# Operand places, order of the first and last pairs, and 512-column products in two halves, in a graph network kernel

## What is computed

```python
h = jnp.maximum(_layernorm(x, axis=-1), 0.0)
x = x + L0(h, adj)       # attention-weighted diffusion, K = 3
h = jnp.maximum(_layernorm(x, axis=-1), 0.0)
x = x + L1(h, adj)       # three graph convolutions
# L0:
Xw = X @ Wv + bv
sj = Xw @ aw[:d, 0]; si = Xw @ aw[d:, 0]
e = leaky_relu(sj[:, None, :] + si[:, :, None] + ab[0], 0.2)
alpha = A * exp(e); transition = alpha / (alpha.sum(-1) + 1e-12)
for k in range(3):
    H = H + Xk @ Wk[k] + bk[k]
    Xk = transition @ Xk
return relu(H)
# L1, three times (relu but for the last):
out = adj @ (x @ W) + b
```

## Time and profile before

| | us |
|---|---|
| median of 3 runs | 844.22 (843.95 to 844.86) |
| profiled execution | 844.0 |
| its span, first to last instruction | 842.2 |
| TensorE busy | 825.1 |
| VectorE busy | 716.8 |
| ScalarE busy | 683.8 |
| GpSimd busy | 506.4 |

### The profile page before, as it was taken

The page is one execution under the profiler, slowest core; times in us unless marked ns, Lnnn a source line. Parts: engine busy times, 40 slices in busy tenths (PEclk is TensorE's granted clock), DMA queues, the critical chain, the costliest instruction groups (busy, mean ns, idle before and its releaser), DMA issues.

```text
span 842.2 us, 20991 instructions
## 1 busy us (share of the span) xinstructions
PE 825.1 (98%) x6214; PEld 777.6 (92%) x6214; DVE 716.8 (85%) x2001; ACT 683.8 (81%) x1675; POOL 506.4 (60%) x591
## 2 busy tenths in 40 slices
PE   8699999999999999999999999999999999999996
PEld 6599999999999999999999999999999999999996
DVE  5788888888888888888888888888889889888872
ACT  3788888888888888888888888888888888888773
POOL 3456655665665665665665665665665665665553
PEclk9999999999999999999999999999999999999999
DMA  6143343343343343343343344344344344334101
GB/s 169 29 114 81 95 114 78 93 114 82 97 106 86 99 101 87 99 99 88 99 97 89 101 96 95 93 97 101 88 97 103 86 96 112 81 92 101 45 26 38
DMA packets 244780, 77.15 MB, mean 92 GB/s; under 512 B 202294, under 2 KB 236859, under 8 KB 244668
## 3 DMA queue, kind: packets, MB, share of 16 engines
q1 hardware_dynamic: 243580, 74.77, 37.2%
q10 hardware_dynamic: 1088, 1.05, 0.4%
HBM read 43.00 MB, written 32.77 MB: 90 GB/s over the span
## 4 chain that ended last, share of the span: by engine, by line
PE 95%; POOL 1%; issue 1%; DVE 1%; ACT 1%; DMA 0%; SPq 0%; ACTq 0%; POOLq 0%; DVEq 0%
PE bank L968 43%; PE bank_p L968 37%; PE bank_turned L968 7%; PE bank_T L968 5%; PE bank_T L991 2%; PE bank_p L1149 1%; POOL w_gcn_lo L425 0%; POOL rstd L381 0%; DMA bv_row<-in_L_gnn_bv 0%; POOL y__lo L390 0%; ACT y_full L612 0%; ACT y_hi L567 0%; DVE y_full L782 0%; DVE stats L680 0%; PE bank_turned L979 0%
## 5 line engine op out<-in xcount | busy, mean ns | idle before, releaser
L390 POOL TENSOR_TENSOR y__lo<-y_full,y__hi 128x256 fp32r<-128x256 f32 x256 | 182.8, 734 | 132.4 <-ACT y_full L612 132.4
L381 POOL TENSOR_TENSOR rstd<-veps,minus_half 128x2 f32<-128x2 f32 x128 | 111.2, 869 | 190.4 <-DVE veps L697 190.4
L968 PE MATMUL bank_p<-w_p_hi,h0T_hi 128*128 128x258 f32 (+1 forms) x512 | 177.7, 363 | 2.5 <-ACT h0T_hi L510 2.5
L968 PE MATMUL bank_p<-w_p_lo,h0T_hi 128*128 128x258 f32 (+1 forms) x512 | 167.4, 342 | 0.0
L968 PE MATMUL bank_p<-w_p_hi,h0T_lo 128*128 128x258 f32 (+1 forms) x512 | 142.4, 339 | 0.6 <-DVE h0T_lo L674 0.6
L968 PE MATMUL bank<-w_gcn_hi,y__hi 128*128 128x256 f32 x512 | 130.8, 290 | 1.6 <-ACT y__hi L612 1.3
L968 PE MATMUL bank<-w_gcn_lo,y__hi 128*128 128x256 f32 x512 | 124.9, 279 | 0.0
L612 ACT ACTIVATE y__hi<-bank,bias_col 128x256 fp32r<-128x256 f32 x256 | 119.9, 468 | 3.1 <-PE bank L968 3.0
L612 ACT ACTIVATE y_full<-bank,bias_col 128x256 f32<-128x256 f32 x256 | 120.7, 472 | 0.0
L968 PEld LDWEIGHTS bank_p<-w_p_hi,h0T_hi 128*128 128x128 f32 x512 | 97.4, 190 | 9.4 <-ACT h0T_hi L510 2.9
L968 PEld LDWEIGHTS bank_p<-w_p_lo,h0T_hi 128*128 128x128 f32 x512 | 97.6, 191 | 5.4
(11 more groups left out here) (104 smaller groups left out, 2289.7 us busy)
## 6 DMA issues: line engine op xcount, KB each, us to landing
x_in<-in_x SPq DMA_DIRECT2D x64, 256.0 KB, 3.0
x_new<-x_out SPq DMA_DIRECT2D x64, 256.0 KB, 2.2
h_rows<-h SPq DMA_DIRECT2D x61, 256.0 KB, 2.1
h_blocks<-h_rows SPq DMA_DIRECT2D x244, 64.0 KB, 2.5
adj_blocks<-in_adj SPq DMA_DIRECT2D x256, 32.0 KB, 2.0
w_raw<-in_L_gnn_Wk ACTq DMA_DIRECT2D x3, 256.0 KB, 6.0
w_raw<-in_L_gnn_W SPq DMA_DIRECT2D x3, 256.0 KB, 3.5
wv_raw<-in_L_gnn_Wv ACTq DMA_DIRECT2D x1, 256.0 KB, 3.9
```

What stands on the lines that cost most here:

```text
L381: pool.tensor_tensor(rstd[n][k % 2][:], veps[n][k % 2][:], minus_half[:], ALU.pow)\
L390: pool.tensor_tensor(y[n][1][:, c], y_full[n][:, c], plain(y[n][0][:, c]), ALU.subtract)\
L968: return pe.matmul(dst, stationary, moving, start=start, stop=stop, skip_group_check=True)
```

## The change

It does four things.

1. Places: the operands of products are declared first, moving ones from a kilobyte boundary on (a filler tensor ahead of them), stationary ones behind a filler of 64 bytes. The rows of `w_p2` and `p2` become 288 floats wide, of which 258 are used. `scratch` goes; the dot products write their unused result into `x_out`.
2. The first rounds: `aw` and `bv` are spread by the DMA itself; row products and copies go. Pair 1 is normalized and turned in round 0, pair 2 in round 1; the bias rows are spread behind ap; weight cuts, adjacency cuts and statistics of the first pairs move between the first three rounds; counts of `keep_busy` change, and two more calls stand in round 0.
3. The last rounds: for the last pair y1's parts are made before s3's, ay stands before z3, and the identity turns before m and z1 are 8 and 8 for 16 and 8.
4. Each product of 512 columns for p0 and p1 becomes two of 256 with the same stationary block.

```diff
-BUSY_FIRST, BUSY_BEFORE, BUSY_BETWEEN, BUSY_TAIL = 11, 7, 8, 16
+BUSY_FIRST, BUSY_BEFORE, BUSY_BETWEEN, BUSY_SCORES, BUSY_SUMS, BUSY_TAIL = 11, 14, 6, 4, 8, 8
+WIDE = D + P // 4
...
+        sb("up_to_a_kilobyte", [P, 3 * P // 4])
+        w_gcn = [None] + [hilo(f"w_gcn{n}", [P, C, D]) for n in range(1, K)]
+        w_p01 = hilo("w_p01", [P, C, 2 * D])
+        y1 = slots_hilo(2, "y1_", [P, G, D])
+        m = hilo("m", [P, C, G, P])
+        s3 = hilo("s3", [P, G, D])
+        adjT_full = [sb(f"adjT_full{n}", [P, G, P]) for n in range(4)]
+        w_p2 = hilo("w_p2", [P, C, WIDE])
+        p2 = slots_hilo(2, "p2_", [P, G, WIDE])
+
+        sb("half_a_block", [P, P // 8])
+        w_gcn[0] = hilo("w_gcn0", [P, C, D])
+        h0T = slots_hilo(2, "h0T", [P, G, C, P])
+        s2 = sb("s2", [P, G, D])
+        y = [hilo(f"y{n}_", [P, C, G, P]) for n in range(2)]
+        h1 = [sb(f"h1_{n}", [P, G, D]) for n in range(2)]
+        aT = slots_hilo(2, "aT", [P, G, P])
+        adjT = slots_hilo(4, "adjT", [P, G, P])
...
-            sp.dma_start(aw_row[:], aw.rearrange("(o d) x -> o (d x)", o=1)).then_inc(score_rows_in, 16)
-            sp.dma_start(bv_row[:], row(bv)).then_inc(score_rows_in, 16)
+            sp.dma_start(aw_bc[:], aw.rearrange("(h d) o -> o h d", h=2).to_broadcast([P, 2, D]))\
+              .then_inc(score_weights_in, 16)
+            sp.dma_start(bv_bc[:], row(bv).to_broadcast([P, D])).then_inc(score_consts_in, 16)
...
 # SyncE, round 1
+                if second(i):
+                    load_adj_blocks(3, 3)
...
 # GpSimd, one(i, k)
+                if first(i):
+                    power(0, 1, 1)
+                    power(0, 2, 2)
                 if b is not None:
                     power(1, b, k - LAG_B)
-                if b is not None and not second(i):
+                if i == 2:
+                    gcn_weights_low((2,))
+                    adjT_low(0, 0)
+                if b is not None and after(i, 3):
                     adjT_low(b, (k - LAG_B) % ROUND)
...
 # ScalarE, one(i, k)
-                if a is not None and a < ON_TENSOR:
-                    hT_high(a, k)
-                if first(i):
+                if first(i):
+                    hT_high(0, 0)
                     p01_weights_high()
-                    biases_copied()
...
                     exponentials(a, k)
+                    if first(i):
+                        first_norm(1, 1)
+                    if second(i):
+                        hT_high(2, 2)
                     p1_copy(a, k, 0)
...
+                if first(i):
+                    hT_high(1, 1)
+                    gcn_weights_high((0,))
+                    biases_copied()
...
+                if second(i):
+                    first_norm(3, 3)
+                if i == N_PAIRS - 1:
+                    y1_high(a, k)
                 if c is not None and not tail(i):
                     s3_high(c)
+                if a is not None and i < N_PAIRS - 1:
+                    y1_high(a, k)
+                if first(i):
+                    first_norm(2, 2)
...
 # VectorE, round 0
                 x_statistics(1, 1)
+                moments(0, 1, 1, lambda: None)
+                guard_variance(0, 1, 1)
                 turn_adj(0, 0)
+                shift(0, 1, 1)
                 p2_low(0, 0)
-                moments(0, 1, 1, lambda: attention(0, 0))
-                guard_variance(0, 1, 1)
+                attention(0, 0)
                 aT_low(0, 0)
-                shift(0, 1, 1)
+                x_statistics(2, 2)
+                moments(0, 2, 2, lambda: None)
+                guard_variance(0, 2, 2)
+                hT_low(1, 1)
...
                 p0_bias(0, 0)
+                turn_adj(1, 1)
+                x_statistics(3, 3)
...
 # TensorE
-                        last = matmul(bank_p[:, g, :], h0T[k % 2][a][:, g, c, :], w_p01[b][:, c, :],
-                                      c == 0 and (a, b) == (HI, HI), c == C - 1 and a == LO)
+                        for n in range(2):
+                            cols = slice(n * D, (n + 1) * D)
+                            last = matmul(bank_p[:, g, cols], h0T[k % 2][a][:, g, c, :], w_p01[b][:, c, cols],
+                                          c == 0 and (a, b) == (HI, HI) and n == 0, c == C - 1 and a == LO)
...
+                if i == N_PAIRS:
+                    ay_product(b, kb)
                 if d is not None and not tail(i - 1):
                     z3_product(d, kd)
-                if b is not None:
+                if b is not None and i < N_PAIRS:
                     ay_product(b, kb)
...
                 if first(i):
-                    pe.wait_ge(bias_rows_in, 16 * 2)
-                    matmul(bank_3[:, 0:D], ones[:], bk_rows[:], True, True).then_inc(bias_rows_spread, 1)
-                    matmul(bank_3[:, D:2 * D], ones[0:1, :], b3_row[:], True, True).then_inc(bias_rows_spread, 1)
+                    keep_busy(BUSY_SCORES)
                 if a is not None:
                     spread_scores(a, k)
+                if second(i):
+                    turn_h(2, 2)
...
                 if c is not None:
                     z2_product(c, kc)
+                if first(i):
+                    turn_h(1, 1)
...
+                    keep_busy(BUSY_SUMS, bank_2[:, 0:P])
```

More of the change, by code:

```diff
@@ L95, in slots @@
             return [sb(f"{name}{s}", shape, dt) for s in range(n)]
-        def slots_hilo(n, name, shape):
-            return [hilo(f"{name}{s}", shape) for s in range(n)]
         x_in = slots(X_SLOTS, "x_in", [P, G, D])
         adj_blocks = slots(4, "adj_blocks", [P, G, P])
-        adjT_full = slots(4, "adjT_full", [P, G, P])
-        adjT = slots_hilo(4, "adjT", [P, G, P])
         x1b = slots(4, "x1b", [P, G, D])
@@ L348, in one @@
                 turned = here(i, -2) if i >= ON_TENSOR - 2 else None
+                if second(i):
+                    load_adj_blocks(3, 3)
                 if turned is not None:
                     write_rows(turned, turned % ROUND)
-                if (n := here(i, -2)) is not None:
+                if (n := here(i, -2)) is not None and not second(i):
                     load_adj_blocks(n, n % ROUND)
@@ L868, in _ @@
             shift(0, 0, 0)
[L869 to L870 removed]
+            dve.wait_ge(score_weights_in, 16 * 2)
             for c in range(C):
@@ L907, in one @@
                     s3_low(d)
-                if a is not None and a < ON_TENSOR:
-                    hT_low(a, k)
                 if (n := early_norm(i)) is not None:
@@ L920, in one @@
                 if second(i):
-                    turn_adj(a, k)
+                    shift(0, 3, 3)
                 if b is not None:
@@ L972, in turn_h @@
                 pe.wait_ge(norm_made[0], i + 1)
-                if after(i, 2):
-                    pe.wait_ge(m_lo, i - 1)
-                elif not first(i):
+                if not first(i):
                     pe.wait_ge(hT_first_lo, i)
@@ L1008, in h_low_ready, with times_weights @@
                     pe.wait_ge(hT_lo, i - ON_TENSOR + 1)
-            def times_weights(hT, rows, w, dst, starts, passes=(False, True)):
+            def times_weights(hT, rows, w, cols, dst, starts, passes=(False, True)):
                 steps = [(g, c, a, b) for low in passes for g in range(G) for c in range(C)
@@ L1015, in times_weights @@
                     start = c == 0 and a == HI and b == HI and g in starts
-                    last = matmul(dst[g], rows(hT[a], g, c), w[b][:, c, :], start, a == LO and c == C - 1)
+                    last = matmul(dst[g], rows(hT[a], g, c), w[b][:, c, 0:cols], start, a == LO and c == C - 1)
                 return last
@@ L1161, in one @@
                 kb, kc, kd = (k - LAG_B) % ROUND, (k - LAG_C) % ROUND, (k - LAG_D) % ROUND
-                if a is not None and a < ON_TENSOR:
-                    turn_h(a, k)
                 if first(i):
+                    turn_h(0, 0)
                     keep_busy(BUSY_BETWEEN)
@@ L1190, in one @@
                     ap_product(a, k)
+                if first(i):
+                    pe.wait_ge(bias_rows_in, 16 * 2)
+                    matmul(bank_3[:, 0:D], ones[:], bk_rows[:], True, True).then_inc(bias_rows_spread, 1)
+                    matmul(bank_3[:, D:2 * D], ones[0:1, :], b3_row[:], True, True).then_inc(bias_rows_spread, 1)
+                    keep_busy(BUSY_SUMS, bank_2[:, 0:P])
                 if b is not None and tail(i):
```

107 lines of the change are left out of this document (37 added, 70 removed).

## The result

| | before | changed |
|---|---|---|
| median of the runs, us | 844.54 (843.95 to 844.88, 4 runs) | 838.36 (836.86 to 838.93, 4 runs) |
| profiled execution, us | 844.0 | 836.86 |
| its span, us | 842.2 | 834.7 |
| its mean granted clock | 0.996 | 1.000 |

The ratio is 0.993, with a 95% interval of 0.9909 to 0.995: the change saves 6.2 us, where 12.7 were forecast. The first line of the profile page answers to the earlier trace rows. There are 773 more products, nearly all of them the halves, and TensorE is as full as before.

A forecast was written before the change was run, and what follows sets the result against it. TensorE, busy 98% of the span, was taken as the bound, with a second path over aT_hi as long. From 844.0 us, 6.7 (steady rounds), 4.8 (head) and 1.1 (tail) came off: 831.4, say 831.5 us; range 826 to 840.

The forecast's parts named there:

- part (a) of the steady rounds: Operand places in every steady round: all products get z1's places modulo 128, so slow 256-column products fall to about 0.113 us.
- Segment A: Steady round from ap to ay, where TensorE alone decides: better places save 0.11 us per round.
- the first rival: Steady rounds: places do nothing or the 0.118 pace stays, gain 0 to 3 us, 838 to 840 us; chance 0.22.
- the 6.7 us: Forecast gain of the 61 steady rounds, 0.11 us each; bounds 3.1 and 9.2, zero if places are nothing.
- If z3 and ay stay at 0.118, 0.05: Low case for the stretch from ap to ay: z3 and ay unimproved, 0.05 us saved per round.
- Segment B: Steady round from ay to ap (second p2 pass, s2, p0/p1): saves 0.15 us, all given back waiting for aT_hi at ap.
- The third rival: Path over aT_hi moves with TensorE and isn't the bound: ay-to-ap gain counts, 9 us more, 822 us; chance 0.05.
- The split: p0/p1 in steady rounds: 24 products of 256 columns for 12 of 512, weight loads hidden, worth nothing.
- The head: First rounds: spreads at about 13.5, 25.2 and 38 us; 5.4 us worked out, 4.8 taken, bounds 2.5 and 6.
- The second rival: First rounds: the head stays at the half clock, about 834 us; chance 0.11.
- The tail: Last pair: ay and hb move some 1.0 us ahead, saving 1.1 us, bounds 0.5 and 1.4.
- The sum: Whole kernel: 844.0 less 6.7, 4.8 and 1.1 us gives 831.4, say 831.5 us.

The follow-up runs named there:

- filler_192: The changed kernel with a filler of 192 bytes instead of 64 ahead of the stationary operands: 846.26 us, one run, round 12.65 us.
- filler_320: The early_attention kernel with a filler of 320 bytes instead of 64: 836.54 us, round 12.480 us.
- early_attention: The changed kernel, but from round 2 on alpha is made before pair b's shift and aT_hi before its normalization: 835.26 us, 0.9895 of the kernel before.
- no_split: The changed kernel with p0/p1 in 12 whole products of 512 columns again: 837.01 us, 0.993 of the kernel before, round 12.53 us.
- early_unsplit: The early_attention kernel with p0/p1 in 12 products of 512 columns: 837.06 us, 0.9912, round 12.49 us.
- order_only: The changed kernel with the old places and products of 512 columns, only the order of first and last pairs changed: 837.94 us, 0.9941 of the kernel before.
- restart_z3: The early_attention kernel with a wait for s3's low part and two identity turns ahead of z3: 846.62 us, one run, rounds alternating 12.63 and 12.70 us.

## Why the prediction was right and wrong

**The failed step.** It is part (a) of the steady rounds, "z1's places everywhere", and in it the prices "z3 and ay: 0.71 to 0.68 each" and 0.117 for the 258-column products. Segment A was to fall by 0.11 us and fell by 0.02: p2's first pass 0.011, ap's products behind its wait 0.005, z3 and ay together nothing. It is the first rival that came true: 0.118 stays, and the median of 838.36 us lies in the 838 to 840 that this rival gave. The text had the evidence itself, "z3 has z1's places and mostly runs at 0.118". Counted out over the trace of before, z3 runs at 0.1133 in 1 of 53 steady rounds, that of the earlier trace rows, and at 0.117 in 52. The forecast took the exception for what places give and the 52 for an accident of the entry from p2; but z3 still comes behind p2 after the change, and p2 keeps its 258 columns, so the accident was the rule. Of the 6.7 us, 0.9 came.

**"If z3 and ay stay at 0.118, 0.05"**, the lower bound of 3.1 us, was too high as well. It took p2 and ap at 0.117; they have run at 0.119 to 0.121, before and after.

**Places as such** were right in kind and wrong in their measure. With operands that agree modulo 256, z1, s2, s3 and the halves go at 0.120, and a filler of 64 bytes changes that. The Trainium skill's "SBUF — State Buffer", section "Who interferes with whom", has TensorE read its moving operand and its weights through two independent ports and names no such cost; the measurement decides, 853.31 us against 838.36. But the distance counts modulo 256 and not 128 (filler_192, filler_320), so half of p2's and ap's products never got "z1's places", and the state in which a run is entered counts beside it.

**Segment B** was to save 0.15 and give it all back at ap. It saved 0.04 (p0/p1 0.010, s2 0.031), and 0.04 came back in the wait at ap, whose first product takes 0.168 for 0.133. The size failed with the pace: the last six halves and the first three products of s2 run at 0.118. The mechanism was right: hb to ap's load 5.50 us for 5.51, a stall where it was said to be, though 0.05 us and not 0.1 to 0.2, gone when early_attention took the wait away. The third rival, that the path moves with TensorE, falls by this.

**The split** was priced at nothing in a steady round, and no_split and early_unsplit agree: nothing behind the wait, 0.013 without it. The formula of "TensorE: Matmul & The Clock Gate" in the Trainium skill, section "Wait — 56ns, not 53.3ns?", gives 109.2 ns for one 256-column product; no steady run of any kernel here goes below 113.

**The head** was right in its steps and nearly in its size: dots forecast from 6.8 and begun at 6.75; spreads forecast at 13.5, 25.2 and 38 and come at 12.11, 24.74 and 37.51; 5.4 worked out, 4.8 taken, 5.65 measured. The first spread came 1.4 earlier than forecast by something that the forecast didn't name: before, three of VectorE's six dots were stretched to 0.9 to 1.5 us beside GpSimd's cuts, and these stretches went. At the second spread 0.5 of it was left, behind TensorE's waits for the p0/p1 weights (1.49) and for hb (1.51). order_only has the same head in a trace with a full clock (5.8). The size is partly luck: some 1.5 of the 5.65 us is the half clock, which the profiled execution of before had and this one hadn't, so with it the head's gain is some 4.1. The second rival, the half clock in the head, is thus there in part: the other three runs are 1.7 to 2.2 us longer at a lower mean clock, which fits one such stretch, but no trace shows them.

**The tail**: 1.1 forecast, 0.9 measured, 32.3 us from the last spread for the 32 forecast, by the mechanism named (ay and hb 1.04 earlier).

**The sum**: with 0.9 for 6.7 in the rounds, 5.65 for 4.8 and 0.9 for 1.1, the span comes out 7.5 shorter, as it did; the median is 1.5 above the profiled execution, most likely by the clock. The forecast's own mark for being wrong, a round over 12.5, was met.

**What stays open.** What in the entry picks the pace has not been found: restart_z3 alternates between both with the same instructions, so it isn't the product before alone. Whether it is p2's two columns or the places of its second rows that end the pace for z3 is not separated. Nor has any run told where the period of 256 bytes comes from. Why the clock falls in the head of some executions and not of others was not tried either, nor whether GpSimd's cuts are what stretches VectorE's operations.

## What to carry to other kernels

When one shape shows two prices in a trace, collect every place where the favoured case is slow before building on it, and count it over all rounds, since one round can be the one exception in 53. When a change speeds one engine up, find the next path to the same instruction and time it; here 5.50 us from hb to a weight load ate what the faster products gave, and moving two steps of other engines forward in their queues was worth more (some 3 us by the medians, 1.6 between the profiled spans) than places and halves together (0.9 in 61 rounds). Before comparing the first microseconds of two traces, compare their clocks: here one stretch at half clock was worth 1.5 us. A layout is worth a try with a filler of another size, from 0 to 15 us here, but only the run tells which.

## What was unexpected of the hardware

A run of 256-column float32r products, each with its own weight load, goes at one of two steady paces, 0.1133 or 0.118 us per product, at the full granted clock and with nothing waiting; with operands that agree modulo 256 bytes the long runs go at 0.120. In the distances tried, the distance from moving to stationary place modulo 256 says which are open (64, 320 and 576 bytes alike, 192 and 448 alike, to the nanosecond in the round). A run often takes over the pace of the one before it: the same six halves at 0.118 behind plain float32 products and at 0.113 behind their own kind. Behind products of 258 columns z3 lost the fast pace in every round of the changed kernel, but s2 found it again after three products; those of 272 columns passed it on in some rounds, and one kernel alternates between both paces from round to round.
